# Layer-0 attention scores from two float32r parts on half the rows of the array, in place of three bf16 parts on 96 rows

## Chip, cores and metric

One Trainium2 chip, one core. The time is the device time of one launch in microseconds (us), the median of the runs. The kernel computes two transformer layers in one launch. Engines go by their names in the profile: PE is TensorE (PEld its weight loads), DVE is VectorE, ACT is ScalarE, POOL is GpSimd, and SP is the queue that issues the DMAs.

## What is computed

The input has 4 batches of 512 tokens with 256 features. Only the part around the change is shown; the rest (two mixture-of-experts layers, layer 1's chunked attention) stays as it is.

```
# layer 0 attention, per batch, 16 heads of 16 features
q = rope(xn @ Wq.T); k = rope(xn @ Wk.T); v = xn @ Wv.T
memory   = einsum(elu(k)+1, v)              # linear part
scores   = einsum('bhqd,bhkd->bhqk', q, k) / sqrt(16)
attn     = softmax(scores) @ v
combined = sigmoid(gate) * mem_out + (1 - sigmoid(gate)) * attn
x = x + combined @ Wo.T + moe0(xn)
```

The scores need more than bf16 precision, since an exponential follows, so q and k are split into a sum of parts of lower precision, and the products of the parts are added. The parts and their products are stacked along the contraction: head features of part 0, of part 1 and so on lie under each other on the partitions, and one product sums over all of them.

## The kernel before

There are three stages: `layer0_front` (norm, projections, rotation, linear memory and layer-0 experts), `middle` (softmax attention of layer 0, output projection, and the projections and routing of layer 1), and `layer1_main`. The change touches the first two.

**Front.** One chain of steps per batch (norm, transposes, logits, q/k projection, rotation, v projection, features, memory) runs beside 11 expert tiles of the batch before. For batch 0 nothing runs beside it: each engine does its steps in the order of the `steps` table and then starts the tiles. `first`, `rest`, `second`, `third` make the three bf16 parts of q and k: ACT rounds `qk` to `part0` (L479), POOL subtracts it from `qk` (L414), ACT rounds the rest to `part1` (L486), POOL forms `part2` (L423). i = 0 is q, i = 1 is k. On ACT `first(1)` and `second(0)` stand behind `copy_v`, then `copy_kf` (L498, the features of k for the memory product), then `second(1)`, and then the tiles: per tile ACT applies SiLU to the gate product (L452), DVE multiplies by the up product (L528) and by the routing weight (L533), ACT rounds to `hh` (L455), POOL takes the remainder (L402), and PE forms the down product into `a_psO`. On PE the gate and up products of tile t+2 (12 products, `a_psG`) stand ahead of the down product of tile t, and wait for DVE's multiplication of tile t (`mult_done`).

**Middle.** Per batch there are 4 groups of 4 heads. Scores are made twice. Row products (`rows`, L1201, into the two banks of `psM`) have a query on each partition; DVE reduces each to its negative maximum (L1075). The maxima of a group are split in two, transposed (`turn_max`, L1208), copied (L1098), and sent through DRAM into two more rows of `qst`; `kst` has ones there. Transposed products (`scores`, L1219, into the two banks `psE`) have a key on each partition and the maximum already subtracted; ACT takes the exponential (L1006); `values` (L1228, into `psV`) multiplies by v. A group has four slots k = 0..3 (128 keys each). The row products run two groups ahead. In slot k PE issues: scores of heads 0, 1; in slot 1 the `turn_max` of the next group; row products of heads 0, 1; values of slot k-1; scores of heads 2, 3; `beside(k)`, the step that a table gives for this slot of the batch before (14 of 16 slots of a batch have one: heads, transposes, projections); row products of heads 2, 3. Batch 0 has nothing beside it, and the last two groups of batch 3 have no row products. Each engine is in order, so the order written here is the order of the work.

Of the kernel before, what the change touches and what calls it, by code (L numbers as in the profile page):

```python
# [11 lines left out]
F32 = mybir.dt.float32  # L12
# [8 lines left out]
P = 128  # L21
# [17 lines left out]
HSLOTS = 4  # L39
# [11 lines left out]
STACKM = STACK + 2  # L51
# [169 lines left out]
def layer0_front(nc, io, scratch, keep):  # L221
# [3 lines left out]
    with ExitStack() as ctx:  # L225
# [22 lines left out]
        parts = [sb(f"part{i}", [P, 2 * KT, SEQ], BF16) for i in range(3)]  # L248
# [21 lines left out]
        part_done, rest_done = [sem(f"part{i}") for i in range(3)], sem("rest")  # L270
# [68 lines left out]
        def _(sp):  # L339
# [24 lines left out]
            def front(n):  # L364
# [10 lines left out]
                for i in range(3):  # L375
                    sp.wait_ge(part_done[i], 2 * n + 2)
                    sp.dma_start(scratch["parts"][n, i].rearrange("k p n -> p k n"), parts[i][:, :, :]).then_inc(parts_stored, 16)
# [16 lines left out]
            for done, n in ((v_stored, 1), (qf_stored, 1), (parts_stored, 3), (cT_stored, 1)):  # L394
                sp.wait_ge(done, 16 * n * BATCHES)

        @block.gpsimd
        def _(pool):
# [9 lines left out]
            def rest(i):  # L408
                def step(n):
# [6 lines left out]
                return step  # L416

            def third(i):
                def step(n):
                    half = slice(KT * i, KT * (i + 1))  # L420
                    pool.wait_ge(part_done[1], 2 * n + i + 1)
                    pool.wait_ge(parts_stored, 48 * n)
                    nc.gpsimd.tensor_tensor(parts[2][:, half, :], qk[:, half, :], parts[1][:, half, :],  # L423
                                            ALU.subtract).then_inc(part_done[2], 1)
                return step
# [4 lines left out]
            steps = {(0, 0): (power,), (8, 0): (rest(0),), (9, 0): (third(0), rest(1)), (10, 0): (third(1),)}  # L430
# [12 lines left out]
        def _(act):  # L443
# [30 lines left out]
            def first(i):  # L474
                def step(n):
                    half = slice(KT * i, KT * (i + 1))
                    act.wait_ge(rotated, 2 * n + i + 1)
                    act.wait_ge(parts_stored, 48 * n)
                    nc.scalar.activation(parts[0][:, half, :], qk[:, half, :], ACT.Copy).then_inc(part_done[0], 1)  # L479
                return step  # L480

            def second(i):
                def step(n):
                    half = slice(KT * i, KT * (i + 1))
                    act.wait_ge(rest_done, 2 * n + i + 1)
                    nc.scalar.activation(parts[1][:, half, :], qk[:, half, :], ACT.Copy).then_inc(part_done[1], 1)  # L486
                return step
# [1573 lines left out]
```

## Time and profile before

| | |
|---|---|
| median of 3 runs | 1190.88 us (1188.92 to 1192.23) |
| span of the profiled execution | 1186.0 us |
| busy PE / DVE / ACT / POOL | 972.0 / 584.5 / 433.3 / 311.8 us |
| front, about | 0 to 300 us |
| middle, about | 300 to 730 us |
| layer 1 | 730 us to the end |
| mean granted TensorE clock | 0.892 |

The page gives no other time of the profiled execution than its span, from its first to its last instruction; the runs' times contain what lies around it. The span is cut into the stages above by the names of the tiles. A busy PE is not a PE at its peak, because each matmul is shown with its latency, and several are in flight. The granted clock tells which of its two levels (1.2 and 2.4 GHz) the engine ran at: 0.50 is the lower one.

### The profile page before, as it was taken

The numbers are of one execution on the slowest core, as the hardware profiler recorded it, in microseconds if no ns is written. First come the engines' busy times: TensorE is split into PE (matmuls) and PEld (weight loads), VectorE is DVE, ScalarE is ACT, GpSimd is POOL, SyncE is SP. The second block draws the span as 40 slices with busy tenths as digits, with TensorE's granted clock in tenths as the row PEclk, the third lists the DMA queues.
The fourth block names the chain that finished last, engine by engine and source line by source line (L and its number), as shares of the span: only waits on it lengthen the run. The fifth ranks groups of instructions, "written<-read, shape, count | busy, mean of one in ns | idle before, by whom it ended". The sixth has DMA issues, their size and how long they took to land. (4 is left out here: it accounts for less than half of the span.)

```text
span 1186.0 us, 16176 instructions
## 1 busy us (share of the span) xinstructions
PE 972.0 (82%) x5323; PEld 623.9 (53%) x5323; DVE 584.5 (49%) x1221; ACT 433.3 (37%) x662; POOL 311.8 (26%) x217
## 2 busy tenths in 40 slices
PE   3699999999589999999998763259999888999871
PEld 2588888888112334444434552235556555665541
DVE  4556566643577785577573322533233333333335
ACT  3435354452245556647646513002222221222210
POOL 3622425153230002012002121033333333333210
PEclk9989999999679998899898877569999999999975
DMA  6713314240523222412321205994322232333352
GB/s 212 224 36 96 110 54 150 54 151 1 145 62 91 66 79 93 145 59 89 133 65 63 98 32 165 274 286 122 109 77 80 80 77 76 85 78 89 81 175 71
DMA packets 150413, 125.47 MB, mean 106 GB/s; under 512 B 63424, under 2 KB 128080, under 8 KB 150352
## 3 DMA queue, kind: packets, MB, share of 16 engines
q1 hardware_dynamic: 146608, 114.45, 32.4%
q0 software_dynamic: 3744, 10.23, 2.9%
q8 instruction: 36, 0.59, 0.2%
q14 instruction: 25, 0.20, 0.1%
HBM read 85.76 MB, written 38.86 MB: 105 GB/s over the span
## 5 line engine op out<-in xcount | busy, mean ns | idle before, releaser
L1075 DVE TENSOR_REDUCE b_negmax<-b_psM 128x1 f32<-128x512 f32 x256 | 163.2, 683 | 75.6 <-PE b_psM L1201 72.6
L1006 ACT ACTIVATE b_probs<-b_psE 128x512 f32<-128x512 f32 x256 | 138.8, 595 | 118.2 <-PE b_psE L1219 117.3
L1201 PE MATMUL b_psM<-b_kst,b_qst 96*128 96x512 bf16 x256 | 98.5, 432 | 27.6 <-DVE b_negmax L1075 13.7
L1219 PE MATMUL b_psE<-b_qst,b_kst 98*128 98x512 bf16 x256 | 89.8, 410 | 15.4 <-ACT b_probs L1006 10.8
L402 POOL TENSOR_TENSOR a_hh<-a_h,a_hh 128x512 fp32r<-128x512 f32 x44 | 57.7, 1312 | 145.5 <-ACT a_hh L455 145.5
L1580 POOL DMA_INDIRECT scratch_ys<-d_y,d_put x39 | 40.2, 1030 | 178.4 <-ACT d_y L1618 176.8
L1847 PE MATMUL d_psG<-d_w,d_xT 128*128 x156 | 80.7, 642 | 4.1 <-issue 3.2
L1855 PE MATMUL d_psU<-d_w,d_xT 128*128 x156 | 79.9, 638 | 0.0
L1219 PEld LDWEIGHTS b_psE<-b_qst,b_kst 98*128 98x128 bf16 x256 | 20.9, 99 | 107.4 <-ACT b_probs L1006 53.8
L1872 PE MATMUL d_psY<-d_w,d_hidden 128*128 x312 | 76.7, 390 | 0.3 <-ACT d_hidden L1612 0.3
L1228 PE MATMUL b_psV<-b_probs,b_vst 128*32 128x512 f32 x512 | 73.6, 648 | 3.2 <-ACT b_probs L1006 3.2
L1586 POOL TENSOR_TENSOR d_rs<-d_ss,d_neghalf 128x16 f32<-128x16 f32 x16 | 46.8, 2928 | 93.0 <-DVE d_ss L1762 93.0
L1201 PEld LDWEIGHTS b_psM<-b_kst,b_qst 96*128 96x128 bf16 x256 | 24.3, 100 | 84.0 <-DVE b_negmax L1075 60.5
L1872 PEld LDWEIGHTS d_psY<-d_w,d_hidden 128*128 128x128 f32 x312 | 58.7, 194 | 15.5 <-issue 8.9
L1732 DVE TENSOR_TENSOR d_probs<-d_ps,decay 128x512 f32<-128x512 f32 x64 | 43.2, 687 | 43.4 <-PE d_ps L1886 43.1
L528 DVE TENSOR_TENSOR a_h<-a_h,a_psG 128x512 f32<-128x512 f32 x44 | 30.2, 686 | 68.4 <-ACT a_h L452 68.4
L1618 ACT ACTIVATE d_y<-d_psY 128x256 f32<-128x256 f32 x39 | 14.9, 383 | 125.4 <-PE d_psY L1872 125.4
L1727 DVE TENSOR_TENSOR d_hidden<-d_hidden,d_psU 128x512 f32<-128x512 f32 x39 | 26.8, 687 | 67.2 <-PE d_psU L1855 67.0
L1931 PE MATMUL d_ps<-d_ident,d_normed 128*128 128x128 f32 x32 | 8.0, 337 | 61.6 <-DVE d_normed L1770 61.6
L1606 ACT ACTIVATE d_hidden<-d_psG 128x512 f32<-128x512 f32 x39 | 23.3, 597 | 94.2 <-PE d_psG L1847 94.2
L956 POOL TENSOR_TENSOR b_combined<-b_both 128x256 f32<-128x256 f32 x16 | 11.6, 724 | 167.6 <-DVE b_both L1119 167.6
L455 ACT ACTIVATE a_hh<-a_h 128x512 fp32r<-128x512 f32 x44 | 27.8, 632 | 73.7 <-DVE a_h L533 73.7
(310 smaller groups left out, 2174.7 us busy)
## 6 DMA issues: line engine op xcount, KB each, us to landing
scratch_parts<-a_part SPq DMA_DIRECT2D x12, 512.0 KB, 4.0
b_qst<-scratch_parts SPq DMA_DIRECT2D x96, 64.0 KB, 2.3
b_kst<-scratch_parts SPq DMA_DIRECT2D x96, 64.0 KB, 2.3
scratch_parts<-b_part SPq DMA_DIRECT2D x24, 256.0 KB, 3.4
d_qst<-scratch_parts SPq DMA_DIRECT2D x96, 64.0 KB, 2.7
d_kst<-scratch_parts SPq DMA_DIRECT2D x96, 64.0 KB, 2.9
a_cbc<-scratch_cT SPq DMA_DIRECT2D x16, 256.0 KB, 3.9
scratch_v<-a_v SPq DMA_DIRECT2D x4, 1024.0 KB, 4.3
```

Source lines behind the costliest of these rows:

```text
L402: nc.gpsimd.tensor_tensor(hh[s % HSLOTS][1][:, :], h[s % 2][:, :], hh[s % HSLOTS][0][:, :].bitcast(F32), ALU.subtract).then_inc(lo_done, 1)
L1006: nc.scalar.activation(probs[k % PSLOTS][:, h, :], psE[h % 2][:, :], ACT.Exp, scale=float(HD) ** -0.5).then_inc(scores_used[h % 2], 1)
L1075: nc.vector.tensor_reduce(negmax[i][:, t, h:h + 1], psM[:, h % 2, :], AX_X, ALU.max, negate=True).then_inc(rows_used[h % 2], 1)
L1201: nc.tensor.matmul(psM[:, h % 2, :], qst[g][0:STACK, h, t * P:(t + 1) * P], kst[g][0:STACK, h, :], start=True, stop=True).then_inc(rows_re ...
L1219: nc.tensor.matmul(psE[h % 2][:, :], kst[g][0:STACKM, h, k * P:(k + 1) * P], qst[g][0:STACKM, h, :], start=True, stop=True).then_inc(score ...
L1228: mm = nc.tensor.matmul(psV[VW * h:VW * (h + 1), :], vst[g][:, k, VW * h:VW * (h + 1)], probs[k % PSLOTS][:, h, :], start=k == 0, stop=k = ...
L1580: nc.gpsimd.indirect_dma_start(scratch["ys1"], bass.IndirectOffsetOnAxis(ap=put[:, b:b + 1], axis=0), y[b % YSLOTS][:, :], None).then_inc( ...
L1586: nc.gpsimd.tensor_tensor(rs[:, :], ss[:, :], neghalf[:, :], ALU.pow).then_inc(rs_done, 1)
L1732: nc.vector.tensor_tensor(probs[g][:, :], (ps1 if g % 2 else ps0)[:, :], decay[:, HG * g:HG * g + HG, :].rearrange("p h c -> p (h c)"), AL ...
L1847: mm = nc.tensor.matmul(psG[:, :], xT[b % 2][:, k, :], weights(b, GATE + k * H1, H1), start=k == 0, stop=k == KT - 1)
L1855: mm = nc.tensor.matmul(psU[:, :], xT[b % 2][:, k, :], weights(b, UP + k * H1, H1), start=k == 0, stop=k == KT - 1)
L1872: mm = nc.tensor.matmul(psY[:, 0:D], hT[b % 2][:, k, :], weights(b, DOWN + k * D, D), start=k == 0, stop=k == HT1 - 1)
```

## The change

q and k are split into two float32r parts, not three bf16 ones, and three products of parts are summed (hi*hi, hi*lo, lo*hi), not six. They stack to 48 rows of the array (50 with the two rows of the maximum), not 96 (98). Even heads lie on partitions 0 up, odd heads on partitions 64 up, and each product names its half of the array by `tile_position`. In a slot the order is now scores h, rows of the other half, for h = 0..3; then `beside`. `turn_max` comes behind the fourth product of slot 1. The transposes of the maxima are float32, not bf16. `HSLOTS`, the buffers of `hh` in the front, go from 4 to 3.

```diff
-HSLOTS = 4
+HSLOTS = 3
...
+Q_HALF = (0, 0, 1)
+K_HALF = (0, 1, 0)
+ROWS = len(Q_HALF) * HD
+ROWSM = ROWS + 2
+SPLITS = 2
+BAND = 64
...
-                    pool.wait_ge(features, 2 * n + i + 1)
-                    nc.gpsimd.tensor_tensor(qk[:, half, :], qk[:, half, :], parts[0][:, half, :],
-                                            ALU.subtract).then_inc(rest_done, 1)
...
+                    nc.gpsimd.tensor_tensor(parts[1][:, half, :], qk[:, half, :], parts[0][:, half, :].bitcast(F32),
+                                            ALU.subtract).then_inc(part_done[1], 1)
...
-            steps = {(0, 0): (power,), (8, 0): (rest(0),), (9, 0): (third(0), rest(1)), (10, 0): (third(1),)}
+            steps = {(0, 0): (power,), (8, 0): (rest(0),), (9, 0): (rest(1),)}
...
-                     (8, 0): (copy_v, copy_xTf), (8, 1): (first(1), second(0)), (9, 0): (copy_kf,), (9, 1): (second(1),)}
+                     (8, 0): (copy_v, copy_xTf), (8, 1): (first(1),), (9, 0): (copy_kf,)}
...
-        qst = [sb(f"qst{g}", [STACKM, HG, SEQ], BF16) for g in range(GROUPS)]
-        kst = [sb(f"kst{g}", [STACKM, HG, SEQ], BF16) for g in range(GROUPS)]
+        qst = [sb(f"qst{g}", [P, HG // 2, SEQ], F32R) for g in range(GROUPS)]
+        kst = [sb(f"kst{g}", [P, HG // 2, SEQ], F32R) for g in range(GROUPS)]
...
-        psN = ctx.enter_context(nc.psum_tensor("b_psN", [P, SEQ], BF16))
+        psN = ctx.enter_context(nc.psum_tensor("b_psN", [P, SEQ], F32))
...
+        ALTERNATE = (1, 0, 3, 2)
...
+                        if isinstance(b, int) and b == 0 and op == 1 and i == len(order) - 1:
+                            sp.wait_ge(ones, 2 * g + 2)
+                        for c in range(2):
+                            at = BAND * c + i * HD
+                            sp.dma_start(dst[g][at:at + HD, :, :].bitcast(F32), src[c]).then_inc(stack_in[g], 16)
...
-                sp.dma_start(qst[g][STACK:STACKM, :, :],
-                             scratch["max"].rearrange("(a h) t -> a h t", a=2)).then_inc(max_in[g], 16)
+                for c in range(2):
+                    sp.dma_start(qst[g][BAND * c + ROWS:BAND * c + ROWSM, :, :].bitcast(F32),
+                                 scratch["max"].rearrange("(a j c) t -> c a j t", a=2, c=2)[c]).then_inc(max_in[g], 16)
...
-                        nc.tensor.matmul(psE[h % 2][:, :], kst[g][0:STACKM, h, k * P:(k + 1) * P],
-                                         qst[g][0:STACKM, h, :], start=True, stop=True).then_inc(scores_ready, 1)
+                        nc.tensor.matmul(psE[h % 2][:, :], kst[g][band(h, ROWSM), h // 2, k * P:(k + 1) * P],
+                                         qst[g][band(h, ROWSM), h // 2, :], start=True, stop=True,
+                                         tile_position=(BAND * (h % 2), 0)).then_inc(scores_ready, 1)
...
-                    scores(k, (0, 1))
-                    if k == 1 and not (last and g == GROUPS - 1):
-                        turn_max(G + 1, (g + 1) % 2)
-                    if ahead:
-                        rows(*next_rows, (0, 1))
-                    if k:
-                        values(k - 1)
-                    scores(k, (2, 3))
+                    for h in range(HG):
+                        scores(k, (h,))
+                        if ahead:
+                            rows(*next_rows, ALTERNATE[h:h + 1])
+                        if h == 1:
+                            if k == 1 and not (last and g == GROUPS - 1):
+                                turn_max(G + 1, (g + 1) % 2)
+                            if k:
+                                values(k - 1)
                     beside(k)
-                    if ahead:
-                        rows(*next_rows, (2, 3))
```

A load of a group's stacks is 12 DMAs of 64 KB and one of 256 KB both before and after.

ACT, at the start of the front, from the rotation of batch 0 to the first expert tile (`a_part` are the parts, `a_xn` the transposed features of k, `a_h` the first tile). Before:

```order
L493 ACTIVATE a_v<-a_psT 128x64x16
L479 ACTIVATE a_part<-a_qk 128x1024
L486 ACTIVATE a_part<-a_qk 128x1024
L498 ACTIVATE a_xn<-a_psT 128x1024
L486 ACTIVATE a_part<-a_qk 128x1024
L452 ACT_TABLE_LOAD
L452 ACTIVATE a_h<-a_psG 128x512
```

And now:

```order
L483 ACTIVATE a_v<-a_psT 128x64x16
L476 ACTIVATE a_part<-a_qk 128x1024
L488 ACTIVATE a_xn<-a_psT 128x1024
L449 ACT_TABLE_LOAD
L449 ACTIVATE a_h<-a_psG 128x512
```

Both copies of L486 are gone from between the rotation and the first tile.

PE, in the middle, from the values of one slot to the first products of a projection of the batch before (`b_psV` values, `b_psE` transposed scores, `b_psM` row products, `b_psX` with `b_wqk` the projection). Before:

```order
L1208 MATMUL b_psN<-b_identb,b_nmparts 8x128 x4
L1200 REGISTER_ALU
L1201 MATMUL b_psM<-b_kst,b_qst 128x512 x2
L1228 MATMUL b_psV<-b_probs,b_vst 32x512 x4
L1218 REGISTER_ALU
L1219 MATMUL b_psE<-b_qst,b_kst 128x512 x2
L58 MATMUL b_psX<-b_xT,b_wqk 128x512
```

And now:

```order
L1200 MATMUL b_psM<-b_kst,b_qst 128x512
L1208 MATMUL b_psN<-b_ident,b_nmparts 8x128 x4
L1229 MATMUL b_psV<-b_probs,b_vst 32x512 x4
L1218 REGISTER_ALU
L1219 MATMUL b_psE<-b_qst,b_kst 128x512
L1199 REGISTER_ALU
L1200 MATMUL b_psM<-b_kst,b_qst 128x512
L1219 MATMUL b_psE<-b_qst,b_kst 128x512
L1200 MATMUL b_psM<-b_kst,b_qst 128x512
L65 MATMUL b_psX<-b_xT,b_wqk 128x512
```

Two row products moved from behind the projection to ahead of it, and the transposes of the maxima moved from ahead of a pair of row products to behind it.

## Rows read from the trace of the kernel before

**Rows 1.** Busy time by stretch, with granted clock (PEclk), DMA share, GB/s.

```profile
62.00:300.00 238.00, 230.33 (x1351) 201.64 (x1349) 132.04 (x263) 104.53 (x136) 86.33 (x58) 0.98 0.24 77
490.00:582.00 92.00, 85.02 (x461) 40.43 (x460) 62.94 (x136) 56.67 (x84) 12.66 (x9) 0.94 0.32 103
```

**Rows 2.** A costly group of the page: busy, mean ns, idle before and its releaser.

```profile
L1075 DVE TENSOR_REDUCE b_negmax<-b_psM 128x1 f32<-128x512 f32 x256 | 163.2, 683 | 75.6 <-PE b_psM L1201 72.6
```

**Rows 3.** Timeline of PE, 46 to 66 us: start, length, instruction, idle before.

```profile
46.55 0.40 PE L58 MATMUL a_psG<-a_xTf,a_wg 128*128 128x512 f32 x1
...
49.36 1.03 PE L701 MATMUL a_psT<-a_ident,a_rot 128*128 128x128 f32 x8
52.03 2.12 PE L709 MATMUL a_psT<-a_v,a_xn 128*128 128x136 f32 x16 [1.64 <-ACT a_xn L498]
59.13 0.80 PE L58 MATMUL a_psG<-a_xTf,a_wg 128*128 128x512 f32 x1 [4.97 <-DVE a_h L528]
...
64.23 0.28 PE L58 MATMUL a_psO<-a_wd,a_hh 128*128 128x256 f32 x1
```

**Rows 4.** Timeline of ACT, the same stretch.

```profile
50.97 1.01 ACT L498 ACTIVATE a_xn<-a_psT 128x1024 f32<-128x1024 f32 x1
55.39 1.06 ACT L486 ACTIVATE a_part<-a_qk 128x1024 bf16<-128x1024 f32 x1 [3.41 <-POOL a_qk L414]
56.46 1.28 ACT L452 ACT_TABLE_LOAD   x1
57.76 0.60 ACT L452 ACTIVATE a_h<-a_psG 128x512 f32<-128x512 f32 x1
```

**Rows 5.** Timelines of DVE and POOL, the same stretch.

```profile
54.20 0.50 DVE L597 TENSOR_TENSOR mem<-a_psT,a_headmask 128x136 f32<-128x136 f32 x2 [6.23 <-PE a_psT L709]
59.18 0.69 DVE L533 TENSOR_TENSOR a_h<-a_h,a_cbc 128x512 f32<-128x512 f32 x1
...
53.23 2.12 POOL L414 TENSOR_TENSOR a_qk<-a_qk,a_part 128x1024 f32<-128x1024 f32 x1
60.61 1.28 POOL L402 TENSOR_TENSOR a_hh<-a_h,a_hh 128x512 fp32r<-128x512 f32 x1 [1.97 <-ACT a_hh L455]
```

**Rows 6.** Timeline of batch 0 in the middle, one slot of 3.52 us.

```profile
345.95 1.07 PE L1228 MATMUL b_psV<-b_probs,b_vst 128*32 128x512 f32 x8
346.95 0.61 PE L1219 MATMUL b_psE<-b_qst,b_kst 98*128 98x512 bf16 x2
347.39 0.60 PE L1201 MATMUL b_psM<-b_kst,b_qst 96*128 96x512 bf16 x2
347.81 2.64 DVE L1075 TENSOR_REDUCE b_negmax<-b_psM 128x1 f32<-128x512 f32 x4 [1.04 <-PE b_psM L1201]
...
349.15 0.10 PEld L1201 LDWEIGHTS b_psM<-b_kst,b_qst 96*128 96x128 bf16 x1 [0.50 <-DVE b_negmax L1075]
349.47 1.07 PE L1228 MATMUL b_psV<-b_probs,b_vst 128*32 128x512 f32 x8
```

**Rows 7.** The same timeline where the maxima are transposed and copied (slot 1).

```profile
356.15 0.39 PE L1208 MATMUL b_psN<-b_identb,b_nmparts 128*8 128x128 bf16 x4
...
356.64 0.41 DVE L1098 COPY b_nmT<-b_psN 8x512 bf16<-8x512 bf16 x1
```

**Rows 8.** Timeline where a projection stands beside a slot (batch 2).

```profile
538.94 0.59 PE L58 MATMUL b_psX<-b_xT,b_wqk 128*128 128x512 f32 x1
```

**Rows 9.** Weight loads, bf16 and float32 (groups by form: busy, mean ns).

```profile
L1219 PEld LDWEIGHTS b_psE<-b_qst,b_kst 98*128 98x128 bf16 x256 | 20.9, 99 | 107.4 <-ACT b_probs L1006 53.8 <-issue 48.9
...
L60 PEld LDWEIGHTS a_psG<-a_xTf,a_wg 128*128 128x128 f32 x88 | 17.4, 198 | 4.1
```

**Rows 10.** Row products alone at the start of the middle; the wait behind them; values of a later slot.

```profile
308.00:332.00 24.00, 19.59 (x37) 3.69 (x38) 21.18 (x36) 9.18 (x25) 5.32 (x4) 0.50 0.60 165
...
332.38 4.23 DVE L1083 CAST b_nmparts<-b_negmax 128x16 bf16<-128x16 f32 x1
...
341.15 1.94 PE L1228 MATMUL b_psV<-b_probs,b_vst 128*32 128x512 f32 x8
```

More of the change, by code:

```diff
@@ L247, in layer0_front @@
         rot = sb("rot", [P, 2 * KT, SEQ])
-        parts = [sb(f"part{i}", [P, 2 * KT, SEQ], BF16) for i in range(3)]
+        parts = [sb(f"part{i}", [P, 2 * KT, SEQ], F32R) for i in range(SPLITS)]
         v32 = sb("v32", [P, TILES, HEADS, VW])
@@ L269, in layer0_front @@
         sined, rotated, min_done, exp_done, features = (sem(n) for n in ("sined", "rotated", "min", "exp", "features"))
-        part_done, rest_done = [sem(f"part{i}") for i in range(3)], sem("rest")
+        part_done = [sem(f"part{i}") for i in range(SPLITS)]
         v_stored, qf_stored, parts_stored, cT_stored = (sem(n) for n in ("v_st", "qf_st", "parts_st", "cT_st"))
@@ L393, in _ @@
                 front(b + 1)
-            for done, n in ((v_stored, 1), (qf_stored, 1), (parts_stored, 3), (cT_stored, 1)):
+            for done, n in ((v_stored, 1), (qf_stored, 1), (parts_stored, SPLITS), (cT_stored, 1)):
                 sp.wait_ge(done, 16 * n * BATCHES)
@@ L477, in step @@
                     act.wait_ge(rotated, 2 * n + i + 1)
-                    act.wait_ge(parts_stored, 48 * n)
+                    act.wait_ge(parts_stored, 16 * SPLITS * n)
                     nc.scalar.activation(parts[0][:, half, :], qk[:, half, :], ACT.Copy).then_inc(part_done[0], 1)
[L480 to L486, printed above, removed]
                 return step
@@ L765, in middle @@
         negmax = [sb(f"negmax{i}", [P, TILES, HG]) for i in range(2)]
-        nmparts = [sb(f"nmparts{i}", [P, TILES, 2, HG], BF16) for i in range(2)]
-        nmT = [sb(f"nmT{i}", [2 * HG, SEQ], BF16) for i in range(2)]
+        nmparts = [sb(f"nmparts{i}", [P, TILES, 2, HG], F32R) for i in range(2)]
+        nmT = [sb(f"nmT{i}", [2 * HG, SEQ], F32R) for i in range(2)]
         outT = sb("outT", [P, GROUPS, SEQ])
@@ L898, in attend @@
                 if not (last and g == GROUPS - 1):
[L899 removed]
+                    send_max(GROUPS * b + g + 2, (g + 1) % GROUPS, (g + 1) % 2, MAX_IN * (b + 1))
                 if g == 1:
@@ L981, in _ @@
             for g in range(GROUPS):
-                nc.gpsimd.memset(kst[g][STACK:STACKM, :, :], 1.0).then_inc(ones, 1)
-            pool.wait_ge(ones, GROUPS)
+                for c in range(2):
+                    nc.gpsimd.memset(kst[g][BAND * c + 32:BAND * c + ROWSM, :, :].bitcast(F32), 1.0).then_inc(ones, 1)
+            pool.wait_ge(ones, 2 * GROUPS)
             norm.setup(pool)
@@ L1071, in reduce @@
             def reduce(n, i, t):
-                for h in range(HG):
-                    dve.wait_ge(rows_ready, 16 * n + HG * t + h + 1)
+                for at, h in enumerate(ALTERNATE):
+                    dve.wait_ge(rows_ready, 16 * n + HG * t + at + 1)
                     nc.vector.tensor_reduce(negmax[i][:, t, h:h + 1], psM[:, h % 2, :], AX_X, ALU.max,
@@ L1194, in _, with band @@
         def _(pe):
+            def band(h, rows):
+                return slice(BAND * (h % 2), BAND * (h % 2) + rows)
             def rows(n, g, t, b, heads):
-                if t == 0 and heads[0] == 0:
+                if t == 0 and heads[0] == ALTERNATE[0]:
                     pe.wait_ge(stack_in[g], LOADED * (b + 1))
@@ L1357, in _ @@
             for t in range(TILES):
-                rows(0, 0, t, 0, range(HG))
-            pe.wait_ge(identb_done, 1)
+                rows(0, 0, t, 0, ALTERNATE)
+            pe.wait_ge(ident_in, 16)
             for t in range(TILES):
-                rows(1, 1, t, 0, range(HG))
+                rows(1, 1, t, 0, ALTERNATE)
                 if t == 0:
                     turn_max(0, 0)
-            pe.wait_ge(ones, GROUPS)
+            pe.wait_ge(ones, 2 * GROUPS)
             def ready():
```

49 lines of the change are left out of this document (19 added, 30 removed).

## The prediction, on record before the changed kernel was run

> **What bounds the kernel now.** I read the busy time by stretch first. From 62 to 300 us PE is busy 230.3 of 238 us [rows 1]: the front, once it runs, is as long as its matmuls, and what other engines save there is hidden. In the middle one batch takes 92 us, with PE busy 85.0, DVE 62.9 and ACT 56.7 [rows 1]. That looks like PE too, but a busy PE here is partly latency, so I read next what the costliest groups waited for. DVE's row maxima idle 72.6 us for row products [rows 2], and ACT's exponentials idle likewise for scores: PE, DVE and ACT take turns. What a slot costs is a chain through all three, so the timelines decide, not the sums.
>
> One slot of batch 0 shows the chain [rows 6]. Values run 1.00 us (345.95 to 346.95); two scores take 0.44; the row product starts at 347.39 and its maximum at 347.81, 0.42 later; two maxima of about 0.65 pass until the bank of the last row product is free at 349.15; that product and a change to the columns of the values take 0.32; values again at 349.47. Sum 1.00 + 0.44 + 0.42 + 1.34 + 0.32 = 3.52. Of the eight products only three stand in it, the others lie under DVE or ACT.
>
> **Term 1, the start of the front.** Batch 0 passes alone through a chain of steps. PE idles 4.97 us before 59.13, for DVE's multiplication, and that waits for ACT's SiLU at 57.76 [rows 3, 4]. ACT was late because both roundings of the second part stand ahead of it, the last at 55.39 after 3.41 us of waiting behind POOL's subtraction (53.23 + 2.12) [rows 4, 5]. The change removes both roundings and both of POOL's third-part subtractions. Then the copy of the features of k can start when PE's transposes end, at 49.36 + 1.03 = 50.39; it ends at 51.4, 0.5 earlier, and the table load of 1.28 ends at 52.7, SiLU at 53.3. Next late is PE's memory product (52.03 + 2.12, now 0.5 earlier), for whose copy DVE waits [rows 3, 5]: DVE is free at 54.2, multiplies until 54.85, and PE starts tile 2 at 54.9, not 59.13: 4.2 us. The 12 products of tile 2 took 64.23 - 59.13 = 5.1 us, at the low level of the clock that PE had fallen to in the idle time; at the high level the same 12 took 49.36 - 46.55 = 2.8 us [rows 3]. With 1.3 us of idle time instead of 5 I take the high level: 2.3 us more. The down product then waits for: weighting 0.69, rounding 0.63, remainder 1.28 [rows 5] and gaps, 54.85 + 2.8 = 57.7, as late as PE itself. First down product at 57.8 to 58.0, not 64.23: -6.2 us. Bounds: -4.2 (clock low all the same) and -6.6. Behind it the front is bound by PE, so this reaches the end. POOL's and ACT's work that goes in batches 1 to 3 lies under PE: 0. `HSLOTS` 3: a rounding at slot j waits for the down product of tile j-3, which PE issues ahead of tile j; only at the batch's first tile does it stand one tile product later, 1.4 us, under the 2.0 us of SiLU and multiplications: 0.
>
> **Term 2, batch 0 of the middle.** In a plain slot the row product of the other half goes beside the first score, so its maximum starts about 0.4 us earlier; the new weights take twice as long to load, 198 against 99 ns [rows 9], which the two products that wait for a bank pay with some 0.1 each: 3.52 becomes 3.3. But once in a group of four slots the maxima are transposed, and DVE's copy of them waits. The transposes now stand behind two row products that themselves wait for DVE, and are float32: DVE stands idle until they are done, with 0.45 for the four of them instead of 0.23, and a copy of 0.69 instead of 0.41 [rows 7]; 0.69 is what another pass over 512 float32 columns takes [rows 5]. I followed a group with these numbers: the slot in which the maxima turn grows by 0.35, the one behind it by 0.13, a plain one shrinks by 0.2, and the last, bound by ACT, stays. Sum +0.3, four groups +1.2. Bounds: -3 (no added latency) to +3.
>
> **Term 3, batches 1 to 3.** Row products of heads 2, 3 stood behind `beside` and now stand ahead of it. They wait for DVE; PE is in order, so the projections wait with them. Where the projection follows the split of x, PE began the projection at 538.94 [rows 8], just as DVE came to the next maxima. Now the last row product must wait for two maxima, 0.74 + 0.60 us later, behind a turn and copy that are 0.9 us late themselves: projection at about 542. Against this, all four products behind the projection find free banks and take about 0.55 where they had taken some 2 us, so the values come only about 1.6 us late. Following one batch in this way, I find the values of the slots at -0.3 to +0.9 us in the first two groups, and +0.9 to +2.2 in the last two; then in the first slots of the next batch, where DVE's long splits had been the bound and PE idled, 2 us of that come back. Sum per batch +0.5 (bounds -6 to +5), three batches +1.5.
>
> Every slot with work beside it also has two changes of the array's tiling more. A change shows as the step from a last product to the values, 0.32 against 0.22 between products [rows 6], so 0.1 each, in the above. The Trainium skill (TensorEngine Tiling (Array Packing), Key Properties) says that a change of tiling mode drains the engine; the trace agrees with 0.1 us. By that rule alone, with nothing hidden, 2 x 0.1 x 42 slots would be +8 us, and it is inside the bounds here. The skill's TensorE: Matmul & The Clock Gate, Weight-path perf modes, has fast weight load only for types other than FP32; the trace's 99 against 198 ns agrees.
>
> **Term 4.** The last two groups of batch 3 have no row products to run beside; 8 slots with 0.1 more each: +0.8. At the start of the middle the row products are alone and each waits for DVE, with some 0.15 more in 16 pairs, 2.4 us; but DVE's next instruction there took 4.23 us, held up until 336.6 by other work [rows 10]. The queues: the load has as many DMAs, `send_max` one more of 0.4 us, with 2 us of room: 0.
>
> **Sum.** -6.2 + 1.2 + 1.5 + 0.8 = -2.7: a span of 1183.3, from 1186.0. The median of the runs is 4.9 us above that span, so 1188.2.
>
> **Rivals.**
> - *PE is the bound after all.* For: 85 of 92 us. In a slot with work beside it eight products take 8 x 0.22 = 1.75 us; two fours take 2 x 0.55, and two changes 0.2: 0.45 less. If half of 42 x 0.45 shows, it is -9.5 in place of +1.5: 1177. Against: the waits of rows 2.
> - *Slower: the clock.* In batch 0 PE would be issuing 1.7 us of a slot of 3.3, 52%, where it was 2.6 of 3.52. At the start of the middle row products alone, 0.86 us of each 1.40 at the low level, left the clock at 0.50 for 24 us [rows 10]. If PE stays at or falls to the low level in batch 0, values take 1.94 in place of 1.00 [rows 10] and a slot some 0.85 us more: 16 x 0.85 = +14, so 1202. It decides if the share of time at which the clock falls lies above a half. Against: from 345 to 398 nothing fell at 73%, and no row shows it between.
> - *The halves don't overlap*: the change doesn't do what it says. Then each product costs 0.22 and part of its longer load, say 0.04 x 8 x 42 = +13: 1201. Against: the eight float32 matmuls of the values, on different columns, take 1.07 us together [rows 6], less than eight of 0.22.
> - *The start gives less*, because the norm of batch 1 or the routing weights are late: 1192.
>
> **Chances.** Forecast 0.42 (own range 1184.5 to 1192; 0.13 of it below the line), PE-bound 0.24, clock 0.18, no overlap 0.09, weaker start 0.07. The line for what a measurement can tell is 0.3%, 3.6 us: 1187.3 and 1194.5. Faster 0.13 + 0.24 = 0.37; the same 0.29 + 0.04 = 0.33; slower 0.18 + 0.09 + 0.03 = 0.30. The range 1177 to 1201 reaches to the rivals on both sides and leaves out about 0.2.
>
> **What would show it.** The first `a_psO` product near 58 us and no idle time of 5 us before it; starts of a score and a row product within 0.05 us; values in batch 0 about 3.3 us apart in plain slots and 0.35 more than before where the maxima turn; projections of batches 1 to 3 starting up to 3 us later behind the values; a granted clock near 1.00 in batch 0. It is wrong if a batch of the middle takes under 89 or over 94 us, or if batch 0 runs at 0.50.

## The result, and the profile after

The changed kernel takes 1250.24 us (1239.88 to 1264.07, four runs) against 1191.56 us for the kernel before beside it: a ratio of 1.0457, 95% interval 1.0409 to 1.0505. The forecast was 1188.2 in a range of 1177 to 1201. It was wrong by 62 us, and on the other side. The median of runs leaves nothing out, the ratio leaves out runs that lie over 1.5% above the fastest of their kernel; for kernels with much time at the low clock that happens often, and they are compared below by their fastest runs where it matters.

The span went from 1186.0 to 1247.2 us. I cut it at the first and the last product of the values. Before the first: 341.2 us, now 339.5 (-1.7). From there to the last: 331.7, now 392.6 (+60.9). Behind it: 513.1, now 515.1 (+2.0). So the loss is in the middle, and the middle by batch shows what it is. The kernel before, one line for each batch (stretch, length, busy time and count of PE, PEld, DVE, ACT, POOL, then the granted clock, DMA share and GB/s):

```profile
341.15:403.38 62.23, 56.38 (x285) 15.18 (x284) 46.24 (x81) 35.99 (x65) 0.00 (x0) 0.98 0.24 72
403.38:498.38 95.00, 88.11 (x462) 42.57 (x461) 62.28 (x136) 56.67 (x84) 12.66 (x9) 0.91 0.26 80
498.38:590.10 91.72, 84.98 (x461) 40.22 (x461) 62.99 (x137) 56.67 (x84) 12.66 (x9) 0.94 0.31 103
590.10:672.90 82.80, 72.15 (x397) 36.91 (x396) 39.02 (x93) 51.38 (x77) 12.63 (x9) 0.92 0.24 81
```

The changed kernel, the same four batches, and ahead of them the stretches that answer to [rows 1] and [rows 10]:

```profile
62.00:300.00 238.00, 227.74 (x1326) 199.92 (x1324) 128.31 (x251) 98.84 (x129) 73.35 (x53) 0.97 0.27 89
308.00:332.00 24.00, 20.16 (x33) 8.29 (x33) 20.25 (x33) 9.18 (x25) 6.83 (x4) 0.50 0.55 153
...
339.50:416.80 77.30, 68.37 (x285) 26.74 (x284) 47.53 (x80) 36.16 (x65) 0.00 (x0) 0.65 0.22 64
416.80:531.62 114.82, 104.52 (x461) 56.06 (x460) 65.99 (x135) 57.64 (x84) 12.65 (x9) 0.72 0.20 61
531.62:637.28 105.66, 92.14 (x461) 49.16 (x460) 65.87 (x135) 57.80 (x84) 12.65 (x9) 0.86 0.29 91
637.28:732.10 94.82, 84.87 (x397) 45.54 (x396) 40.86 (x93) 52.26 (x77) 12.62 (x9) 0.79 0.22 73
```

The counts of PE are the same, and the busy times of DVE and ACT are within 4 us a batch; but the granted clock is 0.65 to 0.86 where it was 0.91 to 0.98, and PE's busy time rises with it. Over the middle it is 0.76 against 0.93: about 188 of 392.6 us at the lower level, 1.2 GHz (2 x 0.24 x 392.6), against about 46 of 331.7. The clock falls in batch 0, at 355.5 us, out of a stretch in which PE was busy 13.07 of 15.5 us (340.0 to 355.5) and never waited over 1.03 us, and comes back only at 399.8.

Groups of the changed kernel's page, which answer to [rows 2] and [rows 9] (busy, mean ns, idle before and its releaser):

```profile
L1004 ACT ACTIVATE b_probs<-b_psE 128x512 f32<-128x512 f32 x256 | 142.7, 596 | 157.6 <-PE b_psE L1219 155.0
L1073 DVE TENSOR_REDUCE b_negmax<-b_psM 128x1 f32<-128x512 f32 x256 | 164.6, 684 | 61.9 <-PE b_psM L1200 61.6
L1200 PE MATMUL b_psM<-b_kst,b_qst 48*128 48x512 f32 x256 | 136.7, 607 | 25.2 <-DVE b_negmax L1073 13.5
L1219 PE MATMUL b_psE<-b_qst,b_kst 50*128 50x512 f32 x256 | 125.7, 563 | 28.4 <-ACT b_probs L1004 28.4
L1219 PEld LDWEIGHTS b_psE<-b_qst,b_kst 50*128 50x128 f32 x256 | 51.8, 232 | 131.2 <-ACT b_probs L1004 65.8
```

DVE waits less for row products than before, 61.6 us against 72.6, since each row product now stands by its score. But ACT waits 155.0 us for scores. Weight loads take 232 ns on the mean over both levels, against 99.

The start of the front, PE, which answers to [rows 3] (start, length, instruction, idle before):

```profile
55.85 0.50 PE L65 MATMUL a_psG<-a_xTf,a_wg 128*128 128x512 f32 x1 [1.19 <-DVE a_h L518]
...
58.77 0.36 PE L65 MATMUL a_psO<-a_wd,a_hh 128*128 128x256 f32 x1
```

And ACT, which answers to [rows 4]:

```profile
51.45 1.02 ACT L488 ACTIVATE a_xn<-a_psT 128x1024 f32<-128x1024 f32 x1 [0.65 <-PE a_psT L691]
52.50 1.28 ACT L449 ACT_TABLE_LOAD   x1
53.79 0.60 ACT L449 ACTIVATE a_h<-a_psG 128x512 f32<-128x512 f32 x1
```

The second roundings are gone, SiLU comes at 53.79 and the first down product at 58.77, 5.5 us earlier than before. PE's idle time before tile 2 is 1.19 us and the 12 products run at the high level, 2.9 us.

One plain slot at the high level, which answers to [rows 6]:

```profile
343.90 1.06 PE L1229 MATMUL b_psV<-b_probs,b_vst 128*32 128x512 f32 x8
...
344.89 0.50 PE L1219 MATMUL b_psE<-b_qst,b_kst 50*128 50x512 f32 x1
...
344.90 0.73 PE L1200 MATMUL b_psM<-b_kst,b_qst 48*128 48x512 f32 x2
...
346.08 0.49 PE L1219 MATMUL b_psE<-b_qst,b_kst 50*128 50x512 f32 x1 [0.44 <-ACT b_probs L1004]
...
347.23 0.64 PE L1229 MATMUL b_psV<-b_probs,b_vst 128*32 128x512 f32 x4
```

Score and row product of different halves start within 0.01 us, and the slot takes 3.33 us, as forecast (3.3). Now a slot 16 us later, at the low level:

```profile
359.99 1.93 PE L1229 MATMUL b_psV<-b_probs,b_vst 128*32 128x512 f32 x8
...
361.85 0.79 PE L1219 MATMUL b_psE<-b_qst,b_kst 50*128 50x512 f32 x1
...
361.85 1.22 PE L1200 MATMUL b_psM<-b_kst,b_qst 48*128 48x512 f32 x2
...
364.78 1.93 PE L1229 MATMUL b_psV<-b_probs,b_vst 128*32 128x512 f32 x8
```

The same slot takes 4.79 us, 1.46 more: the values 0.87 more, the pairs the rest. Where the maxima turn (answers to [rows 7]):

```profile
354.77 0.60 PE L1208 MATMUL b_psN<-b_ident,b_nmparts 128*8 128x128 f32 x4
...
355.48 0.68 DVE L1096 CAST b_nmT<-b_psN 8x512 fp32r<-8x512 f32 x1 [1.19 <-PE b_psN L1208]
```

Transposes of 0.60 and a copy of 0.68, DVE idle 1.19 us ahead of it: the slot takes 5.3 us against 4.94 before.

### The profile page after: what moved, and what is told of

Same layout as the page of the kernel before. It is cut to its first block and busy times, and to the rows that moved or that the text cites. A ratio compares the mean times of both kernels' runs of the same rounds, so it can differ in the third digit from the quotient of the medians.

```text
span 1247.2 us, 16169 instructions
## 1 busy us (share of the span) xinstructions
PE 1025.3 (82%) x5323; PEld 677.3 (54%) x5323; DVE 593.1 (48%) x1220; ACT 428.7 (34%) x654; POOL 295.0 (24%) x213
## 5 line engine op out<-in xcount | busy, mean ns | idle before, releaser
L1004 ACT ACTIVATE b_probs<-b_psE 128x512 f32<-128x512 f32 x256 | 142.7, 596 | 157.6 <-PE b_psE L1219 155.0
L1073 DVE TENSOR_REDUCE b_negmax<-b_psM 128x1 f32<-128x512 f32 x256 | 164.6, 684 | 61.9 <-PE b_psM L1200 61.6
L1200 PE MATMUL b_psM<-b_kst,b_qst 48*128 48x512 f32 x256 | 136.7, 607 | 25.2 <-DVE b_negmax L1073 13.5
L1219 PE MATMUL b_psE<-b_qst,b_kst 50*128 50x512 f32 x256 | 125.7, 563 | 28.4 <-ACT b_probs L1004 28.4
L1219 PEld LDWEIGHTS b_psE<-b_qst,b_kst 50*128 50x128 f32 x256 | 51.8, 232 | 131.2 <-ACT b_probs L1004 65.8
L1229 PE MATMUL b_psV<-b_probs,b_vst 128*32 128x512 f32 x512 | 91.5, 796 | 5.2 <-ACT b_probs L1004 5.2
L1200 PEld LDWEIGHTS b_psM<-b_kst,b_qst 48*128 48x128 f32 x256 | 54.6, 235 | 56.9 <-DVE b_negmax L1073 42.4
```

What stands on the lines that cost most here:

```text
L1004: nc.scalar.activation(probs[k % PSLOTS][:, h, :], psE[h % 2][:, :], ACT.Exp, scale=float(HD) ** -0.5).then_inc(scores_used[h % 2], 1)
L1073: nc.vector.tensor_reduce(negmax[i][:, t, h:h + 1], psM[:, h % 2, :], AX_X, ALU.max, negate=True).then_inc(rows_used[h % 2], 1)
L1200: nc.tensor.matmul(psM[:, h % 2, :], qst[g][band(h, ROWS), h // 2, t * P:(t + 1) * P], kst[g][band(h, ROWS), h // 2, :], start=True, stop= ...
L1219: nc.tensor.matmul(psE[h % 2][:, :], kst[g][band(h, ROWSM), h // 2, k * P:(k + 1) * P], qst[g][band(h, ROWSM), h // 2, :], start=True, sto ...
L1229: mm = nc.tensor.matmul(psV[VW * h:VW * (h + 1), :], vst[g][:, k, VW * h:VW * (h + 1)], probs[k % PSLOTS][:, h, :], start=k == 0, stop=k = ...
```

## The experiments

Theory A: products that span few of the array's rows let the clock fall, and that is the loss. Theory B: the new order costs it. Theory C: the overlapping pairs leave PE less busy, and that lets the clock fall. Theory D: float32r does it. "Middle" is from the first product of the values to the last.

**1. The new order alone** (on the kernel before):

```diff
-                    scores(k, (0, 1))
...
-                    scores(k, (2, 3))
+                    for h in range(HG):
+                        scores(k, (h,))
+                        if ahead:
+                            rows(*next_rows, ALTERNATE[h:h + 1])
```

> The kernel before with the new order of issue alone (one score product, then one row-maximum product, reduced in the order 1, 0, 3, 2); products stay bfloat16 on 98 and 96 rows, nothing overlaps. Theory A (the low TensorE clock comes from products that fill only half the array's rows): granted clock of the middle stays near 0.93, time 1186 to 1200 us. Theory B (the new order costs the time, through later exponentials and reductions): 1225 to 1255 us. Theory C (the clock falls because overlapping pairs leave TensorE less busy): as A, 1186 to 1200.

Measured 1197.73 us, ratio 1.0044 (1.0011 to 1.0077). B is out as the main cause: the order costs about 5 us (1 to 9 by the interval). By batch:

```profile
340.00:399.79 59.79, 55.41 (x288) 15.87 (x287) 44.99 (x80) 36.48 (x66) 0.00 (x0) 0.98 0.25 74
399.79:499.75 99.96, 87.21 (x464) 43.54 (x463) 63.67 (x135) 57.77 (x85) 12.64 (x9) 0.90 0.23 72
499.75:597.57 97.82, 85.25 (x464) 41.76 (x463) 63.70 (x135) 58.07 (x85) 12.66 (x9) 0.91 0.31 99
597.57:681.50 83.93, 73.69 (x400) 37.41 (x398) 39.50 (x93) 51.92 (x78) 12.64 (x9) 0.90 0.25 83
```

Batch 0 gains 2.4 us without any overlap, batches 1 to 3 lose 5.0, 6.1 and 1.1. The row products of the page tell why, before and with the new order:

```profile
L1201 PE MATMUL b_psM<-b_kst,b_qst 96*128 96x512 bf16 x256 | 98.5, 432 | 27.6 <-DVE b_negmax L1075 13.7
```

```profile
L1202 PE MATMUL b_psM<-b_kst,b_qst 96*128 96x512 bf16 x256 | 109.9, 432 | 34.9 <-DVE b_negmax L1076 23.8
```

PE waits 10.1 us more for DVE's maxima, with the step beside the slot queued behind it. In the profiled executions the middle is 9.8 us longer; the medians differ by only about half of that, so this split carries a scatter of some 5 us.

**2. The old order on halves** (on the changed kernel, the edit of experiment 1 turned round):

> The changed kernel with the old order of issue (two score products, then two row-maximum products), float32r on halves of the array kept; neighbours still lie in different halves. Theories A and C: the clock of the middle still falls to about 0.7, 1230 to 1260 us. Theory B: the clock is back near 0.93 and the time at 1185 to 1200 us.

Measured 1257.54 us (1239.32 to 1263.30), ratio 1.0471 (1.0383 to 1.0559). The middle:

```profile
337.30:742.20 404.90, 370.29 (x1598) 183.77 (x1600) 214.48 (x443) 201.09 (x310) 37.99 (x27) 0.74 0.23 70
```

The low clock goes with the half products, whatever their order, as A and C expected.

**3. All products on the lower half**, so that nothing overlaps:

```diff
-                return slice(BAND * (h % 2), BAND * (h % 2) + rows)
+                return slice(0, rows)
...
-                                     tile_position=(BAND * (h % 2), 0)).then_inc(rows_ready, 1)
+                                     tile_position=(0, 0)).then_inc(rows_ready, 1)
```

> The changed kernel with all score and row-maximum products on the lower half of the array (rows 0 to 49), so that none can overlap; odd heads then read the even heads' operands, which changes the values computed and not the work. Theory A (rows used decide): the clock of the middle stays low (0.6 to 0.75), and without the overlap the time is above the changed kernel's, 1255 to 1290 us. Theory C (TensorE's busy time decides): busy time is back at that of the kernel before, clock near 0.93, 1188 to 1205 us.

Measured 1304.69 us (1275.92 to 1324.61), above even the range of A.

```profile
338.20:790.80 452.60, 432.51 (x1597) 232.78 (x1600) 223.36 (x443) 207.88 (x310) 37.91 (x27) 0.67 0.20 63
```

PE is busy 96% of the middle, more than in any kernel with a high clock, and the clock is 0.67. (This is the execution of 1306.16 us. Over the whole launch its clock was 0.805, and that of the fastest run 0.832, against 0.887 in the median for the kernel before beside it.) From 338 to 352 us PE is busy without a gap, 14 of 14 us, and the clock stays at 0.50. C is out: it isn't that PE had become idle.

**4. The same products over rows 0 to 113**, both heads of a pair in one:

```diff
-                return slice(BAND * (h % 2), BAND * (h % 2) + rows)
+                return slice(0, BAND + ROWSM)
```

The upper half of `kst` holds zeros where the changed kernel has its ones: a first form, with ones in both halves, gave exponentials that are not finite, and no time.

> The changed kernel with every score and row-maximum product over rows 0 to 113 (both heads of a pair summed, which changes the values computed and not the number of products): float32r, new order, no overlap, nearly all rows used; it differs from the kernel with all products on the lower half (rows 0 to 49, 1304.69 us) in the number of rows alone. Theory A (rows used decide over the clock): clock of the middle near 0.93, 1185 to 1205 us. Theory D (float32r products as such let the clock fall, whatever rows they use): clock 0.6 to 0.75 and 1270 to 1310 us.

Measured 1211.11 us, ratio 1.0139 (1.0090 to 1.0187).

```profile
342.10:695.40 353.30, 317.90 (x1597) 182.35 (x1600) 220.25 (x443) 204.41 (x310) 38.02 (x27) 0.93 0.26 81
```

float32r, the new order, no overlap, and the clock is that of the kernel before. D is out. The time is 6 us above the range of A: a high clock doesn't bring the whole loss back.

**5. Is it the rows or what they hold?** As 4, with rows 64 to 113 of both operands set to zero (`qst` still gets the maxima in rows 112 and 113, where `kst` is zero):

```diff
-                        for c in range(2):
+                        for c in range(1):
                             at = BAND * c + i * HD
...
+                nc.gpsimd.memset(kst[g][BAND:BAND + ROWSM, :, :].bitcast(F32), 0.0).then_inc(ones, 1)
...
+                nc.gpsimd.memset(qst[g][BAND:BAND + ROWSM, :, :].bitcast(F32), 0.0).then_inc(ones, 1)
```

> As the kernel with all score and row-maximum products over rows 0 to 113, but rows 64 to 113 of both operands hold zeros: the products are those of the kernel on rows 0 to 49 alone (1304.69 us), odd heads again from the even heads' operands, with 64 idle-valued rows beside them. If the number of rows that a product spans decides over the clock, whatever they hold: clock of the middle near 0.93, 1200 to 1220 us. If the data in them decide: clock 0.65 to 0.75, 1280 to 1310 us.

Measured 1207.81 us (1200.04 to 1213.15), ratio 1.0112 (1.0077 to 1.0147).

```profile
334.60:690.60 356.00, 321.45 (x1597) 184.88 (x1600) 219.80 (x443) 204.43 (x311) 38.02 (x27) 0.92 0.21 67
```

This and experiment 3 have the same order, number of products and columns, and nearly the same numbers to add up: the row products here also take in the two rows of the maxima, and the loads of the upper half are left out. What differs is the rows spanned, 114 against 50, and with them that the products lie on the whole array and not on one half of it. The fastest run of each: 1200.0 against 1275.9, 76 us; over the whole launch these two had clocks of 0.899 and 0.832. For the clock, empty rows count like full ones (0.92 against 0.93). This pair alone doesn't tell rows from the use of a half; the next experiment keeps the halves.

**6. Padding each half to its 64 rows**, pairs still overlapping:

```diff
-                return slice(BAND * (h % 2), BAND * (h % 2) + rows)
+                return slice(BAND * (h % 2), BAND * (h % 2) + BAND)
...
+                    nc.gpsimd.memset(qst[g][BAND * c + 32:BAND * c + BAND, :, :].bitcast(F32), 0.0).then_inc(ones, 1)
```

> The changed kernel with each half-array product over all 64 rows of its half in place of 48 or 50, the added ones holding zeros (in the row-maximum products two hold the last batch's maxima, which changes values and not work); pairs still overlap. If spanned rows decide: the clock of the middle rises from 0.76 to 0.80 to 0.88 and the time falls to 1215 to 1240 us. If the added rows don't count because of what they hold: 0.76 and 1245 to 1260 us.

Measured 1225.80 us (1222.66 to 1228.14), ratio 1.0259 (1.0217 to 1.0301), 24 us less than the changed kernel (17 by the fastest runs) for 14 to 16 rows more, which hold nothing of use. The halves, the overlap, the order and the number of products are those of the changed kernel.

```profile
338.30:707.60 369.30, 322.18 (x1601) 166.79 (x1600) 216.74 (x443) 204.23 (x310) 37.91 (x27) 0.86 0.25 77
```

The clock goes from 0.76 to 0.86 with the rows alone. So working on halves isn't the whole cause; whether it has a part in what is left, 0.86 against 0.93, isn't shown.

**7. Fewer rows on the kernel before**, bfloat16 and old order:

```diff
-                    nc.tensor.matmul(psM[:, h % 2, :], qst[g][0:STACK, h, t * P:(t + 1) * P], kst[g][0:STACK, h, :],
+                    nc.tensor.matmul(psM[:, h % 2, :], qst[g][0:STACK // 2, h, t * P:(t + 1) * P], kst[g][0:STACK // 2, h, :],
...
-                        nc.tensor.matmul(psE[h % 2][:, :], kst[g][0:STACKM, h, k * P:(k + 1) * P],
-                                         qst[g][0:STACKM, h, :], start=True, stop=True).then_inc(scores_ready, 1)
+                        nc.tensor.matmul(psE[h % 2][:, :], kst[g][64:STACKM, h, k * P:(k + 1) * P],
+                                         qst[g][64:STACKM, h, :], start=True, stop=True).then_inc(scores_ready, 1)
```

> The kernel before with fewer rows in the products alone: row-maximum products over rows 0 to 47 in place of 0 to 95, score products over rows 64 to 97 in place of 0 to 97 (which drops terms of the sums and no product); bfloat16, the old order, nothing overlaps, nothing else changed. Theory A (rows used decide over the clock): the clock of the middle falls to 0.65 to 0.8 and the time rises to 1235 to 1300 us. Rival E (it takes float32r products on few rows, or the tiles of the changed kernel): clock near 0.93, 1185 to 1200 us.

Measured 1288.03 us, ratio 1.0812 (1.0767 to 1.0857).

```profile
342.80:773.50 430.70, 396.40 (x1601) 157.62 (x1600) 208.66 (x442) 200.68 (x310) 37.95 (x27) 0.64 0.20 66
```

Taking rows away makes the kernel before 97 us slower with no product added: A without float32r and without the new order, with a clock just under its range. A part of the 97 us need not be the clock, since these products lie on halves too, and each change to a product on the whole array costs (experiment 10). One thing that I expected was wrong: the products do overlap. They start at partitions 0 and 64, and in the timeline two of them start together though nothing names their place:

```profile
349.50 0.60 PE L1219 MATMUL b_psE<-b_qst,b_kst 34*128 34x512 bf16 x1
349.51 0.60 PE L1201 MATMUL b_psM<-b_kst,b_qst 48*128 48x512 bf16 x1
```

**8. Buying the clock back.** Further products into the free bank of `psN`, behind three slots of four: two of 128 rows, four of 128 rows, two of 50 rows:

```diff
+            def fill(k, n, G, last_max):
+                pe.wait_ge(nmT_copied, G + 1 if k == 0 or last_max else G + 2)
+                for _ in range(n):
+                    nc.tensor.matmul(psN[:, :], wkv[0][0:P, 0, 0:P], wkv[0][0:P, 0, 0:SEQ], start=True, stop=True,
...
                     beside(k)
+                    if k in (0, 2, 3):
+                        fill(k, 2, G, last and g == GROUPS - 1)
```

> The changed kernel with two more products of 128 rows by 512 columns (on the last layer's weights, result not used) after slots 0, 2 and 3 of each group of the middle, where TensorE waits for an exponential; 96 products in all, about 0.22 us each warm, 0.43 us at the low clock. Theory A: they bring back the clock in part, middle 0.8 to 0.95, 1190 to 1225 us. If rows used don't matter, they only add their own time: 1260 to 1285 us.

> The changed kernel with four further full-height products after slots 0, 2 and 3 in place of two (192 in all). Theory A, with a clock that can be bought back: middle clock 0.88 to 0.95, and the added PE time (about 96 more products of 0.22 us, some 20 us, partly in waits) eats it: 1220 to 1245 us. Rival: the clock stays at 0.86 as with two, 1245 to 1260 us.

> The same two further products after slots 0, 2 and 3, now over 50 rows in place of 128; columns and count as in the kernel with the full ones. Theory A: the clock stays where the changed kernel has it (0.6 to 0.8 in the middle), 1250 to 1285 us, and so over 30 us behind the full-height ones. Rival: what matters is that TensorE is never idle; then both fills give the same time within 5 us.

Measured 1236.26 us (two), ratio 1.0359 (1.0318 to 1.0400); 1238.70 us (four), 1.0407 (1.0343 to 1.0471); 1260.46 us (two of 50 rows), 1.0510 (1.0438 to 1.0582). The middle in this order of kernels:

```profile
338.70:718.30 379.60, 342.63 (x1695) 178.27 (x1694) 217.81 (x443) 204.10 (x310) 37.98 (x27) 0.86 0.24 75
```

```profile
339.60:719.30 379.70, 349.33 (x1789) 187.15 (x1788) 215.11 (x443) 205.14 (x310) 37.97 (x27) 0.90 0.23 75
```

```profile
338.40:744.30 405.90, 374.74 (x1691) 199.69 (x1694) 219.32 (x443) 203.91 (x310) 37.91 (x27) 0.76 0.23 70
```

Useless full-height work makes the kernel about 14 us faster than the changed one (10 by the fastest runs; the intervals of the two ratios, 1.0318 to 1.0400 and 1.0409 to 1.0505, only just part); the same work over 50 rows doesn't. The clock rose as expected, the time didn't come down to the 1190 to 1225 us that I had expected with two. Four of them bring the clock to 0.90 and cost what that gives. The gap between the two kinds, 24 us (14 by the fastest runs), is less than the 30 that I had set.

**9. Half of the change in rows**: scores over 114 rows, row products on halves.

```diff
-                                         qst[g][band(h, ROWSM), h // 2, :], start=True, stop=True,
-                                         tile_position=(BAND * (h % 2), 0)).then_inc(scores_ready, 1)
+                                         qst[g][band(h, ROWSM), h // 2, :], start=True, stop=True).then_inc(scores_ready, 1)
```

> The changed kernel with the score products over rows 0 to 113 (two heads summed, which changes the values) and the row-maximum products left on halves: half of the change in rows. Theory A: a middle clock between those of the kernel with all products tall (0.93) and of the changed kernel (0.76), 0.80 to 0.90, and 1215 to 1250 us. Rival: the clock has a step rather than a slope in this, and the kernel is at one of the two ends, 1205 to 1215 or 1250 to 1290 us.

Measured 1354.15 us (1331.06 to 1376.34). The middle:

```profile
342.40:826.30 483.90, 467.55 (x1601) 222.18 (x1600) 227.04 (x443) 210.60 (x310) 37.98 (x27) 0.73 0.18 59
```

Both are outside everything I had expected. The clock, 0.73, is not between those of the changed kernel (0.76) and of experiment 4 (0.93), though its score products now span 114 rows in place of 50, and the row products still 48. So the number of rows alone doesn't order the clocks, and A in that form is too simple. The timeline shows another cost. Here it is beside that of experiment 4, both at the high level:

```profile
344.10 0.50 PE L1221 MATMUL b_psE<-b_qst,b_kst 114*128 114x512 f32 x1
344.53 0.49 PE L1202 MATMUL b_psM<-b_kst,b_qst 48*128 48x512 f32 x1
344.95 0.51 PE L1221 MATMUL b_psE<-b_qst,b_kst 114*128 114x512 f32 x1
```

```profile
353.54 0.39 PE L1202 MATMUL b_psM<-b_kst,b_qst 114*128 114x512 f32 x1
353.77 0.40 PE L1220 MATMUL b_psE<-b_qst,b_kst 114*128 114x512 f32 x1
354.00 0.39 PE L1202 MATMUL b_psM<-b_kst,b_qst 114*128 114x512 f32 x1
```

A step from a whole-array product to a half one, or back, is 0.42 to 0.43 us; between like ones it is 0.23. So 0.2 us a change, and each of the eight products of a slot pays it. The weight load shows where it goes: between like products it starts under the product before (353.31, for the product at 353.54), here it starts only with its own product, and takes 0.18. That products then pass at about half the rate could be why the clock is low here; no run tests it. The Trainium skill (TensorEngine Tiling (Array Packing), Key Properties) says that a change of tiling mode drains the engine; the trace agrees, with twice the 0.1 us that the prediction had read from the step to the values.

**10. The start's gain without its cause.** The kernel before, with batch 0's two `second` roundings on DVE and POOL's subtractions in the order rest 0, rest 1, third 0, third 1:

```diff
+            at_first[8, 0] = (rest(0), rest(1))
+            at_first[9, 0] = (third(0),)
...
+            at_first[8, 1] = (first(1),)
+            at_first[9, 1] = ()
...
+                    nc.vector.tensor_copy(parts[1][:, half, :], qk[:, half, :]).then_inc(part_done[1], 1)
...
+            at_first[9, 0] = (second(0), second(1))
```

> The kernel before with one part of the change's effect, without its cause: in the start of the front, batch 0 only, the two second roundings go from ScalarE to VectorE (idle there from 48 to 54 us), and GpSimd subtracts rest 0, rest 1, third 0, third 1 in this order. ScalarE is then free for the first SiLU at about 53.5 in place of 57.76 us. My theory that the start's term is real and reaches the end: first a_psO product at 58 to 60 us in place of 64.2, time 4 to 6 us under the kernel before. Rival: the gain is eaten later in the front, within 1 us of the kernel before.

Measured 1189.03 us against 1192.12, ratio 0.9968 (0.9941 to 0.9994), five rounds. It is the fastest of all, though the interval leaves only 0.1% to 0.6% against the kernel before. SiLU and the first down product:

```profile
53.04 0.60 ACT L454 ACTIVATE a_h<-a_psG 128x512 f32<-128x512 f32 x1
```

```profile
59.89 0.36 PE L58 MATMUL a_psO<-a_wd,a_hh 128*128 128x256 f32 x1 [1.75 <-POOL a_hh L402]
```

The down product is 4.3 us earlier than in [rows 3], and the time 3.1 us less, just short of the 4 to 6 expected. PE now waits 1.75 us for POOL, which still has two third-part subtractions ahead of the remainder.

## Why the prediction was wrong

**The failed step is the clock, which stands at nothing in the sum.** It was named only as a rival, with batch 0 as its place, and got a chance of 0.18 and 14 us; the lower clock took about 37 us by the estimate below. Three things in it were wrong. First, what it hung on: I wrote that it decides "if the share of time at which the clock falls lies above a half". The runs show that the share isn't it: 96% busy over 50 rows had 0.67, 90% busy over 114 rows had 0.92 (experiments 3 and 5, 432.51 of 452.60 us and 321.45 of 356.00). A low clock makes PE busier by itself, but 14 us without a gap left the clock of experiment 3 where it was. The one row I held against it, 73% of batch 0 with no fall, was of products with 96 and 98 rows, and I took it over to products with 48 and 50. The kernel before already spoke against a rule of the busy share. Two stretches of its middle, in batch 0 and in batch 1:

```profile
350.00:400.00 50.00, 44.72 (x231) 11.27 (x224) 39.00 (x68) 29.86 (x54) 0.00 (x0) 1.00 0.27 81
450.00:500.00 50.00, 46.67 (x237) 23.75 (x233) 27.58 (x65) 32.21 (x46) 7.21 (x5) 0.83 0.29 95
```

Only in the second does the clock fall, after 452 us; and just ahead of it, from 444 to 452 us, at the high level, PE was busy 7.53 of 8 us, 94%, against 89% in the first. The middle of the kernel before had some 46 us at the low level, and the prediction didn't ask what brought them. The Trainium skill (TensorE: Matmul & The Clock Gate, Why this matters for your kernels) lays drops in mid-kernel to gaps in which PE idles; here the clock fell with no wait over 1.03 us, so the trace does not agree. Second, where: I priced 16 slots of batch 0, and batches 1 to 3 fell too, although the projections beside their slots are whole-array products. Third, the size in a slot: 0.85 us, for the values alone; measured 1.46, since the pairs and what waits for them stretch as well.

The sum with the right sizes: a group of four slots takes 20.72 us at the low level (values at 355.30 and 376.02) and about 15.25 at the high one (354.37 to 369.62, with two further products each behind three slots of it, in the first kernel of experiment 8). About 142 us more at the low level (188 - 46) then lose 142 x (1 - 15.25 / 20.72), about 37 us. The rest of the 60.9 is the new order, 9.8 (experiment 1), and what experiment 4 adds to it, 353.3 - 341.5 = 11.8, which I put down to longer weight loads, float32 transposes and copies. Together 59. This is an estimate: the parts come from different kernels, the ratio is that of batch 0 and is taken over to batches 1 to 3, the 9.8 carries the scatter of experiment 1, and the weight loads, transposes and copies were not tested one by one.

The same sum tells what the overlap bought. Without the 37 us the changed kernel's middle would be about 355 us, and that of experiment 4, which has no overlap at all, is 353.3. In a group at the high level the overlap takes 0.2 us from one slot (3.55 to 3.33), the others are set by DVE's and ACT's chains. At a clock held as before, the change would still have cost some 24 us in the middle (355.6 - 331.7), where terms 2 to 4 add up to 3.5, and the kernel would be near 1213 us, still above the range of 1177 to 1201. So the clock isn't the only thing that failed; the other is term 3, below. The overlap came as described, and was nearly worthless.

**Term 1**, -6.2: right. Measured -5.5: the copy of the features began at 51.45 and not at 50.39, since PE's transposes ended later, and SiLU came 0.5 us later than forecast. Only 1.7 of it is left at the first product of the values. The last down product of the front is 2.3 us earlier, and in two kernels with the same front (experiments 3 and 8, two fills) it is 4.1 and 3.9 earlier, so the missing part isn't fixed; "reaches the end" was too sure.

**Term 2**, batch 0 +1.2: about right where the clock was held. The plain slot is 3.33 us against a forecast of 3.3, the last one 2.76 against 2.7, the one of the maxima 5.3 against 5.3, and batch 0 of experiment 5, though without overlap, is 63.3 us (334.6 to 397.9) against 62.2. A group with overlap at the high level (the 15.25 above, with its further products) is 0.6 over the 14.64 of the kernel before (values at 357.07 and 371.71), where 0.3 was forecast. In the changed kernel itself it is 77.3.

**Term 3**, +0.5 a batch: wrong in size. The new order alone cost 5.0, 6.1 and 1.1 in the profiled execution, 12.2 for a term of 1.5. I had found row products waiting for DVE ahead of the projections, and gave most of it back through the values behind them; the page has 10.1 us more waiting for DVE and no such return.

**Term 4**, +0.8 at the end: not told apart, the last batch mixes it with the clock (its last stretch is 94.8 us against 82.8).

**The rivals.** PE-bound (1177) was wrong: where the clock is high, PE's savings from overlap didn't show. The halves did overlap. The weaker start was in part right, 1.7 us at the middle for -6.2.

## What to carry to other kernels

A product's price on TensorE isn't its columns alone. Before packing or shrinking the contraction of products that fill much of a stage, price the stage with the clock at its low level, and test it on the chip with one cheap edit: the same products over more rows, padded with zeros, which here gave back 24 us for the overlapping halves and 76 us where nothing overlapped (the 76 with the step from a half to the whole array). And look for a side effect of a large change that can be had without it: moving two roundings to an idle engine kept most of the start's gain.

## What the chip showed that I had not expected

- Rows spanned go with the granted clock in all kernels but one: 114 rows 0.92 to 0.93, two halves of 64 rows 0.86, halves of 48 and 50 rows 0.76 (0.74 in the old order), one half 0.67, bfloat16 halves of 34 and 48 rows 0.64. Zeros in the rows count as much as data (0.92 against 0.93). The exception is products of 114 and of 48 rows in turn, 0.73. Why two overlapping halves count less than one whole product, and why this one has so low a clock, stays open.
- The low clock came with no wait of PE over 1.03 us before it, and in another kernel with PE 96% busy.
- Changing between a half-array and a whole-array product costs 0.2 us each time (steps of 0.42 to 0.43 us against 0.23).
- Products whose operands start at partitions 0 and 64 and which have 48 and 34 rows run beside each other without being told to (experiment 7).
